# Attention values turned in 32x32 blocks by VectorE, and GELU's high part made by a second GELU on ScalarE

## The reference

```python
# layer 0                                  # layer 1
x = x + gate_sa * proj(self_attn(mod(ln(x))))   # x = x + self_attn(rope, adaln(x)) @ sa_out_w.T
x = x + proj(cross_attn(ln(x), context))        # x = x + cross_attn(rope, adaln(x), context) @ ca_out_w.T
h = gelu(mod(ln(x)) @ fc1_w + fc1_b)            # h = gelu(adaln(x) @ ffn_w1.T + ffn_b1)
x = x + gate_ff * (h @ fc2_w + fc2_b)           # x = x + h @ ffn_w2.T + ffn_b2
# attention: softmax(q k^T / 4) v per head; everything is float32
```

## Time and profile before

| quantity | value |
|---|---|
| time, median of 3 runs | 1627.46 us (1625.62 to 1627.52) |
| profiled execution, from its first to its last instruction (span) | 1627.8 us |
| busy: PE, PEld | 1478.1 us (91%), 1288.7 us (79%) |
| busy: DVE, ACT, POOL | 1130.2 us (69%), 957.0 us (59%), 721.2 us (44%) |
| mean granted TensorE clock | 0.978 |

### The profile page before, as it was taken

The page is one execution under the profiler, slowest core; times in us unless marked ns, Lnnn a source line. Parts: engine busy times, 40 slices in busy tenths (PEclk is TensorE's granted clock), DMA queues, the critical chain, the costliest instruction groups (busy, mean ns, idle before and its releaser), DMA issues.

```text
span 1627.8 us, 44574 instructions
## 1 busy us (share of the span) xinstructions
PE 1478.1 (91%) x17632; PEld 1288.7 (79%) x17632; DVE 1130.2 (69%) x2407; ACT 957.0 (59%) x1754; POOL 721.2 (44%) x982
## 2 busy tenths in 40 slices
PE   5989999999999999999998989889899897988987
PEld 4768888787888878788787877878778786887867
DVE  5556766666776766667777776866867777687664
ACT  3456565656656565666655655556655565655543
POOL 3133424333342434336557464464644636356321
PEclk9989999999999999999999999999999999999998
DMA  6110100101010010110112000000000001000000
GB/s 221 45 47 10 37 25 29 41 13 56 10 47 15 29 41 29 40 31 24 36 45 66 12 18 15 14 28 11 18 15 15 27 12 31 5 11 15 2 14 14
DMA packets 34251, 49.38 MB, mean 30 GB/s; under 512 B 3488, under 2 KB 24928, under 8 KB 34048
## 3 DMA queue, kind: packets, MB, share of 16 engines
q1 hardware_dynamic: 33760, 46.01, 9.0%
q10 hardware_dynamic: 288, 0.52, 0.1%
HBM read 38.08 MB, written 8.45 MB: 29 GB/s over the span
## 4 chain that ended last, share of the span: by engine, by line
PE 70%; DVE 16%; issue 7%; ACT 4%; POOL 2%; SPq 0%; DMA 0%; DVEq 0%; POOLq 0%; ACTq 0%
PE score_t L677 8%; PE score L656 8%; PE p_mix L719 7%; PE p_unit L746 6%; PE p_unit L550 5%; PE p_unit L551 5%; PE p_unit L552 5%; DVE neg_max L1120 4%; PE p_out L550 3%; PE p_out L552 3%; PE p_out L551 3%; PE p_mix L581 2%; DVE k_t L1110 2%; PE p_turn L736 2%; PE p_turn L729 2%
## 5 line engine op out<-in xcount | busy, mean ns | idle before, releaser
L1120 DVE TENSOR_REDUCE neg_max<-score 128x8 f32<-128x1024 f32 x224 | 274.1, 1224 | 121.0 <-PE score L656 105.5
L656 PE MATMUL score<-k_t,q_t 32*128 32x256 f32 x1792 | 252.3, 398 | 32.5 <-DVE q_less L1130 16.5
L677 PE MATMUL score_t<-q_less,k_t 32*128 32x128 f32 x3584 | 267.0, 288 | 1.0 <-ACT probs_t L980 0.7
L677 PEld LDWEIGHTS score_t<-q_less,k_t 32*128 32x128 f32 x3584 | 224.0, 191 | 13.1 <-issue 7.1
L980 ACT ACTIVATE probs_t<-score_t 128x1024 f32<-128x1024 f32 x168 | 172.1, 1025 | 94.3 <-PE score_t L677 82.3
L656 PEld LDWEIGHTS score<-k_t,q_t 32*128 32x128 f32 x1792 | 161.5, 186 | 70.3 <-issue 31.6
L899 ACT ACTIVATE xt<-p_mix,mod_now 128x128 f32<-128x128 f32 x384 | 154.4, 454 | 80.3 <-PE p_mix L581 61.5
L1324 POOL TENSOR_TENSOR xt_lo<-xt,xt_hi 128x256 fp32r<-128x256 f32 x128 | 95.8, 749 | 207.1 <-ACT xt_hi L904 206.3
L746 PE MATMUL p_unit<-w_out,heads_t 128*128 128x256 f32 x512 | 147.0, 410 | 15.0 <-ACT q_t L943 8.2
L550 PE MATMUL p_out<-w_hi,hid_lo 128*128 128x256 f32 x512 | 151.9, 297 | 5.0 <-issue 2.6
L1167 DVE TENSOR_TENSOR hid_lo<-hid,hid_hi 128x256 fp32r<-128x256 f32 x256 | 141.8, 554 | 8.8
(11 more groups left out here) (161 smaller groups left out, 4349.1 us busy)
## 6 DMA issues: line engine op xcount, KB each, us to landing
ctxt<-in_ctxT SPq DMA_DIRECT2D x16, 512.0 KB, 3.8
side<-gates SPq DMA_DIRECT2D x15, 512.0 KB, 4.6
x_new<-in_x SPq DMA_DIRECT2D x32, 128.0 KB, 2.1
x_mid<-xs SPq DMA_DIRECT2D x8, 512.0 KB, 3.3
x_new<-x_mid SPq DMA_DIRECT2D x32, 128.0 KB, 2.0
out<-xs SPq DMA_DIRECT2D x8, 512.0 KB, 3.2
k_t<-in_L_f_wT SPq DMA_DIRECT2D x2, 1024.0 KB, 5.6
probs_t<-in_L_xcond_fc_w SPq DMA_DIRECT2D x1, 1024.0 KB, 8.8
```

The source lines that it names most:

```text
L656: mm = pe.matmul(score_banks(b, h)[:, r % 2, t * 2 * N:(t + 1) * 2 * N].rearrange("p (e n) -> p e n", e=2), q_t[s][rows(r), t, tokens], k_ ...
L677: mm = pe.matmul(turned_banks(b, h)[:, r % 2, x * N:(x + 1) * N], k_t[s][rows(r), t, e, tokens], q_less[rows(r), j % 2, t, e, :], start=Tr ...
L1120: dve.tensor_reduce(by_half[:, 2 * h:2 * h + 2, 0:CT, :], score_banks(b, h)[:].rearrange("p r (t e n) -> p r t e n", t=CT, e=2), AX.X, ALU ...
```

## The change

Per value, the four transposes there and two back on PE, and the two copies by ACT, are gone. DVE turns `p_mix` in 32x32 blocks into `mix_blocks` (and takes the reciprocal) at step `AT_BLOCKS` = 7 of the value, and at step `AT_HEADS` = 8 it scales and turns the result back in blocks into `heads_t`. `mix_values` writes its columns in runs of 32 in another order, so that the blocks land where they are needed, and some weights and biases are reordered on the way in to fit. The freed bank becomes `p_max`, for the maxima alone, and the waits that shared banks needed are gone. In the MLP, ACT runs the same GELU twice, first into `hid_hi` (whose type rounds), then into `hid`; the DVE cast is gone.

```diff
-PE_ORDER = ("round", "proj", "max", "norm", "mlp", "first", "back", "turn", "unit", "mix")
+PE_ORDER = ("round", "proj", "max", "norm", "mlp", "first", "unit", "mix")
 # PE: turn_max
-                if j == GB:
-                    pe.wait_ge(heads_moved, group * 8 + GB)
-                elif j == GB + 2:
-                    if group:
-                        pe.wait_ge(out_moved, group * 4)
...
-                pe.transpose(max_bank(j)[:, 0:P], neg_max[:, j % 2, :], ident[:]).then_inc(max_turned, 1)
+                pe.transpose(p_max[:, 0:P], neg_max[:, j % 2, :], ident[:]).then_inc(max_turned, 1)
 # PE: mix_values
-                        mm = pe.matmul(p_mix[rows(r), x * N:(x + 1) * N], v_pad[s][:, b, at:at + 32],
-                                       probs_t[j % 2][:, r, x, :], start=True, stop=True, tile_position=(0, 32 * r))
+                        mm = pe.matmul(mix_by_slot[rows(r), x // 2, x % 2], v_pad[s][:, b, at:at + 32],
+                                       probs_t[j % 2][:, r, x, :].rearrange("p (q i) -> p q i", i=32),
+                                       start=True, stop=True, tile_position=(0, 32 * r))
 # PE: turn_heads and turn_back are removed, and
-                if u == 0:
-                    pe.wait_ge(queries_less[1], (group + 1) * 8 + (4 if group < GROUPS - 1 else 0))
 # ACT: move_mix and move_heads are removed; gelu
+                if u >= HID_SLOTS:
+                    act.wait_ge(hid_used, group * HIDDEN + u - HID_SLOTS + 1)
+                act.activation(hid_hi[:, u % HID_SLOTS, :], up_ring[u % 4][:, 0:HALF], ACT.Gelu, bias=bias_cols[:, m:m + 1])\
+                   .then_inc(hid_hi_made, 1)
                 act.activation(hid[:, u % 2, :], up_ring[u % 4][:, 0:HALF], ACT.Gelu, bias=bias_cols[:, m:m + 1])\
                    .then_inc(gelu_made, 1)
 # DVE
+            def turn_blocks(group, j):
+                dve.wait_ge(mixed, group * 8 + j + 1)
+                if not (group == 0 and j == 0):
+                    dve.wait_ge(heads_made, group * 8 + j)
+                dve.transpose(mix_blocks[:], p_mix[:]).then_inc(mix_moved, 1)
+                dve.wait_ge(mix_moved, group * 8 + j + 1)
+                dve.reciprocal(rden[:], mix_blocks[:].rearrange("p (h w) -> p h w", h=H)[:, :, HD]).then_inc(rden_made, 1)
+
             def scale_heads(group, j):
-                dve.wait_ge(turned_q, group * 8 + j + 1)
-                by_head = p_turn[:].rearrange("p (h w) -> p h w", h=H)
-                dve.reciprocal(rden[:], by_head[:, :, HD]).then_inc(rden_made, 1)
                 dve.wait_ge(rden_made, group * 8 + j + 1)
                 if not (group == 0 and j == 0):
-                    dve.wait_ge(turned_back, group * 8 + j)
-                dve.tensor_tensor(heads[:].rearrange("p (h d) -> p h d", h=H), by_head[:, :, 0:HD],
+                    dve.wait_ge(heads_moved, group * 8 + j)
+                dve.tensor_tensor(head_blocks[:].rearrange("p (h d) -> p h d", h=H),
+                                  mix_blocks[:].rearrange("p (h w) -> p h w", h=H)[:, :, 0:HD],
                                   rden[:].unsqueeze(2).broadcast_to([P, H, HD]), ALU.mult).then_inc(heads_made, 1)
+                dve.wait_ge(heads_made, group * 8 + j + 1)
+                if not (group == 0 and j == 0):
+                    dve.wait_ge(projected, group * 8 + j)
+                dve.transpose(heads_t[:].rearrange("p t n -> p (t n)"), head_blocks[:]).then_inc(heads_moved, 1)
 # DVE: split_hidden
-                dve.tensor_copy(hid_hi[:, u % HID_SLOTS, :], hid[:, u % 2, :]).then_inc(hid_hi_made, 1)
 # DVE: body, in front of moments, swap, high keys and row_max
-                        for s, b in batch_at(step, AT_TURN_Q + DVE_SCALE):
+                        for s, b in batch_at(step, AT_HEADS):
                             scale_heads(group, 4 * s + b)
+                    for group, step in live(t):
+                        for s, b in batch_at(step, AT_BLOCKS):
+                            turn_blocks(group, 4 * s + b)
```

More of the change, by code:

```diff
@@ L54 @@
 START = (0, CROSS_FROM)
-AT_TURN_MAX, AT_EXP, AT_MIX, AT_TURN_Q, AT_TURN_BACK, AT_PROJ, AT_STATS, AT_Z, AT_LNT = 2, 3, 6, 7, 8, 9, 10, 11, 11
-ACT_MIX, ACT_UNIT, ACT_MOD, ACT_HI = 0, 0, 0, 0
-DVE_KEYS, DVE_LOW, DVE_SCALE, DVE_SWAP, DVE_OUT = 1, 6, 1, 1, 0
+AT_TURN_MAX, AT_EXP, AT_MIX, AT_BLOCKS, AT_HEADS, AT_PROJ, AT_STATS, AT_Z, AT_LNT = 2, 3, 6, 7, 8, 9, 10, 11, 11
+ACT_UNIT, ACT_MOD = 0, 0
+DVE_KEYS, DVE_SWAP, DVE_OUT = 1, 1, 0
 POOL_ROTATE = 1
@@ L166 @@
                   + [(FIRST_LNT + b, PLACE["first"], "norm", b) for b in range(GB)])
-TURN_BANK = sorted([(at + AT_TURN_Q, PLACE["turn"], "turn", 4 * s + b) for s, b, at in BATCHES]
-                   + [(at + AT_TURN_BACK, PLACE["back"], "back", 4 * s + b) for s, b, at in BATCHES])
 UNIT_BANK = [sorted([(at + AT_PROJ, PLACE["proj"], "proj", 4 * s + b) for s, b, at in BATCHES]
@@ L254, in build_blocks @@
         probs_t = [sb(f"probs_t{n}", [P, ROWS, SLOTS, N]) for n in range(2)]
-        mix_sb = sb("mix_sb", [P, SLOTS * N])
+        mix_blocks = sb("mix_blocks", [P, SLOTS * N])
         rden = sb("rden", [P, H])
-        heads = sb("heads", [P, D])
+        head_blocks = sb("head_blocks", [P, D])
         heads_t = sb("heads_t", [P, CT, N])
@@ L293, in build_blocks @@
         p_mix = bank("p_mix")
-        p_turn = bank("p_turn")
+        p_max = bank("p_max")
         p_unit = bank("p_unit")
         p_out = bank("p_out")
+        mix_by_slot = p_mix[:].rearrange("p (c q e i) -> p c e q i", c=CT, q=N // 32, e=2)
         up_ring = [score_t[:, 0], score_t[:, 1], score[:, 0], score[:, 1]]
@@ L567, in bank_free @@
                     pe.wait_ge(ln_moved[m // GB], (group + d) * 4 + m % GB + 1)
[L568 to L571, removed]
                 elif stage == "proj":
@@ L799, in body @@
                     elif t == MOD_LN_AT:
-                        pe.wait_ge(queries_less[1], 4)
+                        pe.wait_ge(bias_added, 1)
                         modulation_ln()
@@ L822, in body @@
                             turn_z(group, 0, b)
[L823 to L828, removed]
                     for group, step in live(t):
@@ L981, in exps @@
                 op.then_inc(exps_made, 1)
[L983 to L986, removed]
-                act.copy(mix_sb[:], p_mix[:]).then_inc(mix_moved, 1)
-            def move_heads(group, j):
-                act.wait_ge(turned_back, group * 8 + j + 1)
-                if not (group == 0 and j == 0):
-                    act.wait_ge(projected, group * 8 + j)
-                act.copy(heads_t[:].rearrange("p t n -> p (t n)"), p_turn[:, 0:D]).then_inc(heads_moved, 1)
             def split_ctx(group):
@@ L1033, in body @@
                     for group, step in live(t):
-                        for s, b in batch_at(step, AT_TURN_BACK + ACT_HI):
-                            move_heads(group, 4 * s + b)
-                    for group, step in live(t):
                         if step == PRIME_GELU:
@@ L1046, in body @@
                             move_unit(group, UNITS.index(UNIT_AT[layer_of(group)][step - ACT_UNIT]))
-                    for group, step in live(t):
-                        for s, b in batch_at(step, AT_MIX + ACT_MIX):
-                            move_mix(group, 4 * s + b)
             ada_w = a["L0_xcond_ada_w"].rearrange("(t p) n -> t p n", p=P)
@@ L1453 @@
     cos, sin = rope_tables()
+    by_row = np.arange(D).reshape(2, ROWS, 2, HD)[:, :, ::-1].reshape(D)
     by_slot = np.arange(D).reshape(2, ROWS, 2, HD)[:, :, ::-1].transpose(0, 2, 1, 3).reshape(D)
```

19 lines of the change are left out of this document (6 added, 13 removed).

## The result

The changed kernel took 1622.72 us (1618.41 to 1626.43, median of 20 runs), the kernel before 1625.63 in the same jobs (1622.73 to 1627.52): ratio 0.9982, 95% interval 0.9975 to 0.9990. That is 3 us or 0.2% faster, where 1564 had been forecast and 1515 to 1600 as the range.

What follows compares the result with a forecast made beforehand. PE was taken as the bound in most stretches, DVE also in some score steps. PE's transposes and wait, DVE's additions and ACT gave -3.9 and -4.0 us per period, eight each: -63 us, 1564 us, range 1515 to 1600.

Steps and rivals of the forecast that it cites:

- The long one with the MLP has PE at 41.75 ...: taking work from PE shortens it: Layer 0's 43.27 us MLP stretch: PE busy 41.75, DVE 29.11, so less PE work was to shorten it.
- -84.5 us nearly in full: PE's six transposes per value go: 0.66 us each value, 84.5 us over 128 values.
- the term of -5.06 us a period in layer 0 (-4.18 in layer 1): PE's 5.28 us of transposes per period, less those in stretches where PE doesn't set the time.
- DVE's additions: Turning and scaling in stretches with score steps on both sides: +1.27 us per period in layer 0, +1.39 in layer 1.
- So I price it at nothing; if DVE is late, they wait up to 0.74 us: Normed rows' transposes on PE, waiting for DVE to free `p_mix`: priced at nothing, up to 0.74 us four times a period.
- Half of the 43.7 us: PE's wait before the transposes back: half counted as gain, 0.7 us per period in layer 0, 1.85 in layer 1.
- The second GELU at +0.6 us a period: ACT's GELUs in the MLP delay its tail: +0.6 us per period, between 0 and 0.95.
- 8 x (-4.49 - 4.64): Eight periods of both layers: the terms for PE's transposes, PE's wait and DVE's additions, without ACT's +0.6 us.
- rival 2: PE's clock falls in layer 0's last stretch: +2.6 us in up to 8 periods, +21 us, 1585 us; chance 0.09.
- rival 4: DVE becomes the path through the score steps; a loss if over half of 1.33 us per value is exposed: 1662; chance 0.07.
- everything given back to within 0.2%: Whole program: no difference from the kernel before beyond 0.2% (3.3 us); chance 0.03.

Runs made afterwards that it cites:

- pe_work_less: Kernel before with 360 of its 768 transposes on PE (39.6 us) left out, nothing else moved: 1609.47 us, ratio 0.9892.
- no_first_gate: Changed kernel with POOL's gating of layer 0's self-attention output cut to one column: 1617.13 us, ratio 0.9951.

## Why the prediction was wrong, point by point

- **"The long one with the MLP has PE at 41.75 ...: taking work from PE shortens it", and -84.5 us nearly in full.** This step failed: the term of -5.06 us a period in layer 0 (-4.18 in layer 1). By itself such work returns 42% (`pe_work_less`), so the -84.5 us were worth about 35, an estimate from that run. The MLP stretch of layer 0 lost 2.55 us of work and 0.19 of length; turning alone made it 1.2 us longer, and only the GELU half made it shorter. In layer 1 the step held better: the MLP stretch became 3.7 us shorter for 3.2 us less PE, with both halves in place (turning alone 0.7, the GELU alone 1.9). That chains through other engines lay hidden behind PE and appear when PE is shorter is what the waits suggest; it is shown at the place read above, and by `no_first_gate` for a part.
- **DVE's additions.** Their prices held, and so did their sum, though not each stretch (steps 2 to 3: +0.4 and +0.7 us for +0.13 and +0.99; 6 to 7: +0.8 and +0.6 for +0.99 and +0.29; 22 to 23: 0 for +0.15 and +0.11): +1.2 us a period in both layers for +1.27 and +1.39. That the scaling came out at the mean of 554 ns is partly luck: half of them took 417 ns or less, and a few long ones make the mean. What the forecast left out is what the additions do outside these three stretches. It had 8 x (-4.49 - 4.64) = -73 us for turning alone; it measured +33. If PE's part is -35 us, the rest of turning cost some 68 us, 41% of the 165 us that it puts on DVE (91.1 + 70.9 + 57.0 - 54.4). Runs that take parts of that away give 23% and 38%.
- **"So I price it at nothing; if DVE is late, they wait up to 0.74 us".** The hold on `p_mix` stood with 23.0 us among the waits, up to 1.6 us at a time, up to 3.8 with a later place. At the place read above DVE was late by another's fault: its queue stood at POOL's results. Whether that is so at all 29 was not read.
- **Half of the 43.7 us.** The wait went completely, and more came instead: 25.4 + 23.0 + 13.0 (row maxima) + 6.1 (keys) = 67.5 us.
- **The second GELU at +0.6 us a period.** Wrong in sign: +10 us forecast, -19 alone and -36 with turning. I had named the 6.5 us of casts that leave DVE each period and counted them as relief nowhere.
- **The clock, rival 2.** Its mechanism is there, at other places than it said: the share at 1.2 GHz grew from 72 to 127 us, worth some 28 us of PE's busy time by my arithmetic. No run holds the clock fixed, so how much of the 60% that is given back is clock and how much waiting stays open; `pe_work_less` gave three fifths back with no lower clock, so there it was not the clock. In its profiled execution 16.6 of the 25 us that did not come off the span are idle time of PE.
- **Slower by DVE as the path, rival 4.** It had the right condition (a loss when over half of the 1.33 us per value is exposed), but at the full price of PE's work. For turning alone it is what happened, with 41% exposed and 42% returned by the estimates above.
- **The outcome itself** had a chance of 0.03, as everything given back to within 0.2%, and no mechanism. It is a sum of +33 and -36 us that happen to be alike, and the forecast had neither.

The Trainium skill's Vector Engine (DVE) Microarchitecture Reference (3.8, the reshape front-end) has the 32x32 transpose at one element per cycle per lane. The trace fits it: 712 ns for 512 columns and 445 for 256 are 267 ns for 256 more columns, the pace of the two-input operation (264). The Trainium skill's SBUF — State Buffer page (SBUF: two separate sides) says that a DVE operation with two SBUF inputs and a GpSimd operation that reads SBUF exclude each other for a whole instruction. The trace agrees: of the 128 scalings the twelve longest (887 to 2573 ns, median of all 417) each began while a two-input operation ran on POOL, and ended 0.3 us after that one.

Open stay: the split between clock and waits in the changed kernel; why layer 0's MLP stretch stays at 43 us, of which the POOL chain explains some 0.5; and why work near the end of DVE's step makes the heads later than work ahead of the maximum does.

## What to carry to other kernels

A busy share of 90% and more is no bound until a run has shown it: take a few per cent of the engine's work out (here 2.7%), leaving all else in place, and see which part returns; here it was some two fifths, for both signs. A new instruction in an in-order queue has to be priced by its place, by what stands in front of it and behind it and what these wait for, and not by its duration alone: the same work placed by step was 32 us faster, and 91 us of DVE work cost 6 or 32. Changes with two halves are best run as halves, since they may cancel, and the better half alone may beat the whole (1603.54 us here). When a wait in the profile's list goes and the time stays, look for the wait that came in its place.

## What was not expected of the hardware

A microsecond in which PE was busy for 0.39 was followed by three to four at 1.2 GHz in layer 0, where the kernel before had none between 110 and 850 us. Taking 84.5 us of transposes from PE went with a granted clock of 0.961 instead of 0.978, and putting as much back with 0.977; taking 39.6 us from the kernel before did not lower it.
